# Layer 0 attention: both maxima of a pair of steps ahead of the subtraction, row sums and row of maxima change steps

## The chip, the cores and the metric

The kernel runs on one core of a Trainium2 chip. Its engines work side by side, each through its own queue in order, and meet at semaphores: PE (TensorE) multiplies, VectorE (DVE) and ScalarE (ACT) work on what PE leaves in PSUM, GpSimd (POOL) works in SBUF, SyncE (SP) issues the transfers. The metric is the device time of one execution in microseconds, lower is better.

## The reference

Two layers, each `x = x + attention(layernorm(x)) * silu(ffn(layernorm(x)))`, on x of 2048 tokens by 128. The change touches the attention of layer 0 alone, with 16 heads of 64:

```python
q = jnp.einsum('bsm,hmd->bhsd', x, kernel[0])      # k, v alike
scores = jnp.einsum('bhsd,bhtd->bhst', q, k) * scale
attn = jax.nn.softmax(scores, axis=-1)
out = jnp.einsum('bhst,bhtd->bhsd', attn, v)
out = jnp.transpose(out, (0, 2, 3, 1)).reshape(b, s, d * h)
out = jnp.einsum('bsf,fm->bsm', out, WO[0])
```

The softmax subtracts from each row of 2048 scores its maximum.

## The kernel before, in words

The two layers run one after the other, each as a chain of stages. `attention_stage` (from line 565) is the stage of the attention, for layer 0 with `bias=False` and for layer 1 with `bias=True`. It works in 64 chunks n: 16 heads of 4 chunks, each with 512 query columns. A chunk is 8 steps s; a step takes 256 keys as two blocks of 128, each 128 x 512 scores in one half of a PSUM tile `st` (two such tiles, used in turn).

The exact maximum of each query row has to be known before its scores are made. So the kernel makes the scores twice. Two chunks ahead (`AHEAD = 2`), a cheap product `maxima(n + 2, s)` (PE, lines 652 and 653) fills the one buffer `jb`, and VectorE reduces it to one maximum per row (line 845). PE may not fill `jb` again until the reduction has read it. At the start of chunk n VectorE's `merge(n + 1)` (line 851) joins the partial maxima; ScalarE's `divide_maxima(n + 1)` (line 772), issued after the exponential of step 2, spreads them into `m4w`; PE's `row(n + 1)` (line 663) turns `m4w` into a row of maxima in the PSUM tile `xb`; ScalarE copies that to `rows` (line 777), where the scores of chunk n + 1 find it.

Within a chunk the scores (line 688) of even steps carry the maximum as a fourth pair of products, and ScalarE takes the exponential straight from PSUM (line 795). For odd steps VectorE subtracts the maximum (`subtract_maxima`, line 865) into the ring `prob` (`room`, six tiles), and ScalarE takes the exponential there (line 788). PE's `values` (line 699), two steps behind, multiply the exponentials with v into `ov`. GpSimd adds up the exponentials for the sum of each row (lines 943, 946, 950), which ends in `total`.

The finish of a chunk runs in the next one, all of it through the one tile `xb`: ScalarE copies `ov` out (line 802, after the exponential of step 1); PE's `sums_of` (line 710) sums `total` over the partitions, VectorE inverts (line 884); PE's `project` (line 719) multiplies with the output weights, and VectorE accumulates into `acc` (line 890). In which step these stand is set by `SUM_STEP`, `ROW_STEP` and `OUT_STEP`, whose first number is that of layer 0: sums at step 3, row at step 5, projection at step 7.

PE's queue of layer 0 goes by pairs of steps, and `between` holds the row, the sums or the projection:

```python
elif s % 2 == 0:
    ahead(n, s)
    scores(n, s)
    scores(n, s + 1)
    ahead(n, s + 1)
    between(n, s + 1)
if s % 2 == 0 and step >= LAG:
    values(*divmod(step - LAG, NS))
    values(*divmod(step - LAG + 1, NS))
```

Of the kernel before, what the change touches and what calls it, by code (L numbers as in the profile page):

```python
# [19 lines left out]
NCH = H * NC  # L20
# [14 lines left out]
BW = S - P + S - QC + QC  # L35
AHEAD = 2
NJ = 8
SUM_STEP, ROW_STEP, OUT_STEP = (3, 3), (5, 1), (7, 5)


class Memory:
# [523 lines left out]
def attention_stage(nc, k, layer, bias=False):  # L565

    with ExitStack() as ctx:
# [23 lines left out]
        row_ready, row_done = m.sem(g + "row_ready"), m.sem(g + "row_done")  # L591
# [4 lines left out]
        sum_ready, rs_done = m.sem(g + "sum_ready"), m.sem(g + "rs_done")  # L596
# [10 lines left out]
        def scratch(n, j):  # L607
            i = NJ * n + j
            return jb[:, :] if i >= FIRST or i % 3 == 2 else st[:, i % 3, :]

        def summed_by(step):
            n, s = divmod(step, NS)
            return pool_adds * n + (1, 1, 2, 2, 3, 4, 5, 6)[s]

        def by_row(step):
            return bias or step % 2 == 0

        @block.sync
        def _(sp):
            for h in range(H):  # L620
                if h >= 1:
                    sp.wait_ge(loaded, 16 * loads * h)
                    sp.wait_ge(low_loaded, 16 * 4 * h)
                if h >= 2:
                    sp.wait_ge(st_read, NS * NC * (h - 1))
                at = slice((h % 2) * S, (h % 2 + 1) * S)
                pr, half = h // 2, slice((h % 2) * DH, (h % 2 + 1) * DH)
                for low in (slice(0, DH), slice(DH, P)):
                    sp.dma_start(qh[low, at], k.qk_high[0, pr][half, :]).then_inc(loaded, 16)
                    sp.dma_start(kh[low, at], k.qk_high[1, pr][half, :]).then_inc(loaded, 16)  # L630
                if bias:
                    sp.dma_start(tab[:, h % 2, :], k.bias_rows(h)).then_inc(loaded, 16)
                if h == 0:
                    sp.wait_ge(loaded, 16 * loads)
                for low in (slice(0, DH), slice(DH, P)):
                    sp.dma_start(ql[low, at], k.qk_low[0, pr][half, :]).then_inc(low_loaded, 16)
                    sp.dma_start(kl[low, at], k.qk_low[1, pr][half, :]).then_inc(low_loaded, 16)

        @block.tensor
        def _(pe):  # L640
# [14 lines left out]

            def row(n):
                pe.wait_ge(m4_done, n + 1)
                if bias and n >= 3:
                    pe.wait_ge(proj_done, n - 2)
                if not bias and n >= 2:  # L660
                    pe.wait_ge(rs_done, n - 1)
                for t in range(4):
                    last = nc.tensor.matmul(xb[:, t * P:(t + 1) * P], m4w[:, t, :], k.ident16[:, :],
                                            start=True, stop=True)
                last.then_inc(row_ready, 1)
# [37 lines left out]

            def sums_of(n):
                pe.wait_ge(folded, n + 1)
                pe.wait_ge(row_done, min(n + (3 if bias else 2), NCH))
                if n >= 1:
                    pe.wait_ge(proj_done, n)
                for q in range(4):
                    last = nc.tensor.matmul(xb[:, q:q + 1], total[:, q * P:(q + 1) * P], k.ones[:, 0:1],  # L710
                                            start=(q == 0), stop=True, skip_group_check=True)
                last.then_inc(sum_ready, 1)
# [11 lines left out]
            for j in range(NJ):  # L724
                maxima(0, j)
            row(0)
            for j in range(NJ):
                maxima(1, j)
# [31 lines left out]
            for s in range(NS - LAG, NS):  # L760
                values(NCH - 1, s)
            sums_of(NCH - 1)
            project(NCH - 1)

# [66 lines left out]
        @block.vector  # L831
        def _(ve):
            def maxima(n, j):
                ve.wait_ge(max_ready, NJ * n + j + 1)
                if bias:
                    i = NJ * n + j
                    if i >= 2:
                        ve.wait_ge(max_done, i - 1)
                    c0 = 2 * QC + (n % NC) * QC + (j // 2) * P - (j % 2) * 2 * QC
                    nc.vector.tensor_tensor_reduce(  # L840
                        out=junk[:, i % 2, :], in0=scratch(n, j), in1=tab[:, n // NC % 2, c0:c0 + 2 * QC][:, ::-1], scale=1.0,
                        scalar=-3.0e38, op0=ALU.add, op1=ALU.max, accum_out=mx[:, j // 2, j % 2:j % 2 + 1])\
                      .then_inc(max_done, 1)
                else:
                    nc.vector.reduce_max(mx[:, j // 2, j % 2:j % 2 + 1], scratch(n, j), AX.X).then_inc(max_done, 1)  # L845

            def merge(n):
                ve.wait_ge(max_done, NJ * n + NJ)
                if n >= 1:
                    ve.wait_ge(m4_done, n)  # L850
                nc.vector.tensor_reduce(m4[:, :], mx[:, :, :], AX.X, ALU.max).then_inc(merged, 1)
                ve.wait_ge(merged, n + 1)

            def subtract_maxima(n, s):
                step = NS * n + s
                ve.wait_ge(st_ready, step + 1)
                if s == 1:
                    ve.wait_ge(row_done, n + 1)
                if step >= RING:
                    ve.wait_ge(pv_done, step - RING + 1)  # L860
                    ve.wait_ge(summed, summed_by(step - RING))
                p = prob[:, step % RING, :].rearrange("p (t q) -> p t q", t=2)
                x = st[:, step % 2, :].rearrange("p (t q) -> p t q", t=2)
                high = rows[:, n % 2, :].unsqueeze(1).broadcast_to([P, 2, QC])
                nc.vector.scalar_tensor_tensor(p, high, -float(MAXROW), x, ALU.mult, ALU.add).then_inc(lowered, 1)  # L865

            def add_bias(n, s):
                step = NS * n + s
                ve.wait_ge(st_ready, step + 1)
                if step >= RING:  # L870
                    ve.wait_ge(pv_done, step - RING + 1)
                    ve.wait_ge(summed, summed_by(step - RING))
                c0 = S - QC + 2 * s * P - (n % NC) * QC
                first = tab[:, n // NC % 2, c0:c0 + QC]
                window = bass.AP(first.tensor, first.offset, [first.ap[0], [P, 2], [1, QC]])
                p = prob[:, step % RING, :].rearrange("p (t q) -> p t q", t=2)
                x = st[:, step % 2, :].rearrange("p (t q) -> p t q", t=2)
                nc.vector.tensor_tensor(p[:, :, ::-1], x[:, :, ::-1], window, ALU.add).then_inc(added, 1)  # L878

            def invert(n):  # L880
                ve.wait_ge(sum_ready, n + 1)
                if n >= 1:
                    ve.wait_ge(proj_done, n)
                nc.vector.reciprocal(rs[:, :], xb[:, 0:4]).then_inc(rs_done, 1)

            def accumulate(n):
                ve.wait_ge(proj_ready, n + 1)
                for q in range(4):
                    a = k.acc[:, (n % NC) * 4 + q, :]
                    last = nc.vector.scalar_tensor_tensor(a, xb[:, q * P:(q + 1) * P], rs[:, q:q + 1], a,  # L890
                                                          ALU.mult, ALU.add)
                last.then_inc(proj_done, 1)

            ve.wait_ge(ones_set, 2)
            for j in range(NJ):
                maxima(0, j)
            merge(0)
            for j in range(NJ):
                maxima(1, j)
            for n in range(NCH):  # L900
                if n + 1 < NCH:
                    merge(n + 1)
                for s in range(NS):
                    if bias:
                        add_bias(n, s)
                    if not by_row(NS * n + s):
                        subtract_maxima(n, s)
                    if n + AHEAD < NCH:
                        maxima(n + AHEAD, s)
                    if s == sum_step and n >= 1:  # L910
                        invert(n - 1)
                    if not bias and s == out_step and n >= 1:
                        accumulate(n - 1)
            invert(NCH - 1)
            if not bias:
                accumulate(NCH - 1)
# [462 lines left out]
```

## Time and profile before

| | |
|---|---|
| median of the runs before | 3075.92 us (3074.8 to 3075.96) |
| the profiled execution | 3079.59 us, its span 3077.9 us, mean granted clock of PE 0.964 |
| busy over the span | PE 91%, VectorE 81%, GpSimd 81%, ScalarE 51% |
| attention of layer 0 | about 201 to 1431 us, chunk after chunk 18.6 us |
| busy in 300 to 400 us, of 100 | PE 97.88, VectorE 83.40, GpSimd 94.82, ScalarE 56.68; granted clock 1.00 |

A row of the timeline is: start, duration, engine, line, operation, tiles written and read, count, and in brackets the idle time of the engine before it with what ended it. Instructions of an engine follow one another a little faster than their durations say, since the end of one overlaps the start of the next; so intervals are read from start to start. Several rows of PE overlap because two products on different halves of the array run together and are pipelined.

### The profile page before, as it was taken

What the parts mean: (1) busy time and instruction counts of PE and PEld (TensorE: products, weight loads), DVE (VectorE), ACT (ScalarE), POOL (GpSimd) and SP (SyncE); (2) the same over time, 40 slices, a digit from 0 to 9 for tenths busy, and PEclk for the clock granted to TensorE, in tenths of its full rate; (3) what the DMA queues carried; (4) which work ended last, traced back from release to release, by engine and by line L of the source; (5) the groups of instructions that cost most, each with busy time, mean ns of one, the idle gap of its engine ahead of it and who ended that gap; (6) DMA issues with size and microseconds to landing.
All of it is one profiled execution on the core that took longest, in us unless ns stands there. A gap on an engine that the chain in (4) does not pass through costs nothing. (4 is left out here: it accounts for less than half of the span.)

```text
span 3077.9 us, 46733 instructions
## 1 busy us (share of the span) xinstructions
PE 2807.8 (91%) x17656; PEld 1147.6 (37%) x17656; DVE 2504.0 (81%) x3379; ACT 1557.4 (51%) x1889; POOL 2502.6 (81%) x1205
## 2 busy tenths in 40 slices
PE   5959999999999999996499599999999999999997
PEld 3413333333333333333354133333333333333332
DVE  6568888888888888874339699999999999999995
ACT  4325555555555555552122255555555555555554
POOL 0009999999999999994339389999999999999997
PEclk9979999999999999997699699999999999999998
DMA  4250111111111111101203501111111111111100
GB/s 109 86 191 22 35 29 28 28 28 28 28 28 28 28 29 28 28 1 38 60 27 137 190 4 52 55 55 55 55 55 55 55 55 55 55 55 55 55 1 14
DMA packets 63825, 155.28 MB, mean 50 GB/s; under 512 B 18017, under 2 KB 33770, under 8 KB 61426
## 3 DMA queue, kind: packets, MB, share of 16 engines
q1 hardware_dynamic: 62578, 150.20, 17.4%
q8 instruction: 141, 2.31, 0.3%
q0 software_dynamic: 1024, 2.10, 0.2%
q14 instruction: 82, 0.67, 0.1%
HBM read 113.34 MB, written 38.93 MB: 49 GB/s over the span
## 5 line engine op out<-in xcount | busy, mean ns | idle before, releaser
L943 POOL TENSOR_TENSOR a_sums<-a_sums,room 128x1024 f32<-128x1024 f32 x512 | 1195.4, 2364 | 83.1 <-ACT room L795 42.5
L699 PE MATMUL a_ov<-room,va 128*64 128x512 f32 x4096 | 994.0, 606 | 0.0
L784 ACT ACTIVATE room<-room,sscale 128x1024 f32<-128x1024 f32 x512 | 588.3, 1149 | 539.3 <-DVE room L878 539.2
L845 DVE TENSOR_REDUCE a_mx<-a_jb 128x1 f32<-128x1024 f32 x501 | 611.9, 1221 | 129.6 <-PE a_jb L653 123.4
L943 POOL TENSOR_TENSOR a_sums<-room 128x1024 f32<-128x1024 f32 x256 | 604.3, 2361 | 116.6 <-ACT room L784 66.8
L840 DVE CUSTOM_DVE_ANT_0 a_junk<-a_jb,a_tab 128x1024 bf16<-128x1024 f32 x501 | 610.5, 1219 | 83.2 <-PE a_jb L653 74.8
L878 DVE TENSOR_TENSOR room<-a_st,a_tab 128x1024 f32<-128x1024 f32 x512 | 622.9, 1217 | 12.4 <-PE a_st L688 10.2
L795 ACT ACTIVATE room<-a_st,sscale 128x1024 f32<-128x1024 f32 x256 | 285.3, 1114 | 360.1 <-PE a_st L688 360.1
L652 PE MATMUL a_jb<-a_kh,a_qh 64*128 64x512 f16 x1002 | 384.9, 384 | 66.1 <-DVE a_mx L840 32.1
L699 PEld LDWEIGHTS a_ov<-room,va 128*64 128x64 f32 x4096 | 248.7, 136 | 409.3 <-issue 372.7
L688 PE MATMUL a_st<-a_qh,a_kh 64*128 64x512 f16 x2048 | 395.6, 383 | 3.0 <-DVE a_mx L840 2.9
L688 PE MATMUL a_st<-a_ql,a_kh 64*128 64x512 f16 x2048 | 390.8, 378 | 0.0
L688 PE MATMUL a_st<-a_qh,a_kl 64*128 64x512 f16 x2048 | 390.6, 378 | 0.0
L865 DVE SCALAR_TENSOR_TENSOR room<-a_rows,a_st 128x1024 f32<-128x1024 f16 x256 | 312.7, 1221 | 92.3 <-PE a_st L688 90.9
L653 PE MATMUL a_jb<-a_kh,a_qh 64*128 64x512 f16 x1002 | 385.1, 384 | 0.0
L788 ACT ACTIVATE room<-room,sscale 128x1024 f32<-128x1024 f32 x256 | 294.0, 1148 | 170.8 <-DVE room L865 170.8
L946 POOL TENSOR_TENSOR a_sums<-a_sums 128x1024 f32<-128x1024 f32 x128 | 302.8, 2366 | 10.1
L688 PE MATMUL a_st<-a_rows,a_lower 64*128 64x512 f16 x1536 | 292.9, 378 | 0.0
L652 PEld LDWEIGHTS a_jb<-a_kh,a_qh 64*128 64x128 f16 x1002 | 93.6, 93 | 465.8 <-DVE a_mx L845 306.3
L688 PEld LDWEIGHTS a_st<-a_qh,a_kh 64*128 64x128 f16 x2048 | 99.8, 94 | 274.0 <-issue 164.1
L950 POOL TENSOR_TENSOR a_total<-a_sums 128x512 f32<-128x512 f32 x128 | 162.5, 1270 | 10.0
L710 PE MATMUL a_xb<-ones,a_total 128*128 128x1 f32 x1024 | 136.4, 254 | 17.3 <-POOL a_total L950 17.3
(219 smaller groups left out, 2642.6 us busy)
## 6 DMA issues: line engine op xcount, KB each, us to landing
a_tab<-bias_line SPq DMA_DIRECT2D x16, 1984.0 KB, 11.0
qk_high<-q_oh SPq DMA_DIRECT2D x32, 512.0 KB, 2.6
qk_low<-q_ol SPq DMA_DIRECT2D x32, 512.0 KB, 3.6
a_qh<-qk_high SPq DMA_DIRECT2D x64, 256.0 KB, 4.5
a_kh<-qk_high SPq DMA_DIRECT2D x64, 256.0 KB, 5.1
a_ql<-qk_low SPq DMA_DIRECT2D x64, 256.0 KB, 7.5
a_kl<-qk_low SPq DMA_DIRECT2D x64, 256.0 KB, 7.8
ex_w<-in_L_ffn_W SPq DMA_DIRECT2D x1, 2048.0 KB, 10.5
```

The source lines that it names most:

```text
L652: nc.tensor.matmul(o[:, 0:QC], qh[0:DH, q0:q0 + P], kh[0:DH, k0:k0 + QC], start=True, stop=True)
L653: nc.tensor.matmul(o[:, QC:2 * QC], qh[DH:P, q0:q0 + P], kh[DH:P, k0 + QC:k0 + 2 * QC], start=True, stop=True).then_inc(max_ready, 1)
L688: last = nc.tensor.matmul(st[:, step % 2, t * QC:(t + 1) * QC], w, x, start=(r == 0), stop=(r == len(rounds) - 1))
L699: last = nc.tensor.matmul(ov[t * DH:(t + 1) * DH, :], k.va[:, 2 * s + t, h * DH:(h + 1) * DH], prob[:, step % RING, t * QC:(t + 1) * QC], ...
L784: nc.scalar.activation(prob[:, r, :], prob[:, r, :], ACT.Exp, scale=k.sscale[:, layer:layer + 1])\
L788: nc.scalar.activation(prob[:, r, :], prob[:, r, :], ACT.Exp, scale=k.sscale[:, 0:1])\
L840: nc.vector.tensor_tensor_reduce(out=junk[:, i % 2, :], in0=scratch(n, j), in1=tab[:, n // NC % 2, c0:c0 + 2 * QC][:, ::-1], scale=1.0, sc ...
L845: nc.vector.reduce_max(mx[:, j // 2, j % 2:j % 2 + 1], scratch(n, j), AX.X).then_inc(max_done, 1)
L865: nc.vector.scalar_tensor_tensor(p, high, -float(MAXROW), x, ALU.mult, ALU.add).then_inc(lowered, 1)
L878: nc.vector.tensor_tensor(p[:, :, ::-1], x[:, :, ::-1], window, ALU.add).then_inc(added, 1)
L943: nc.gpsimd.tensor_tensor(a, first, prob[:, step % RING, :], ALU.add).then_inc(summed, 1)
L946: nc.gpsimd.tensor_tensor(a, a, sums[:, (n + 1) % 2, :], ALU.add).then_inc(summed, 1)
```

## The change

Three things in layer 0. The constants swap the steps of the sums and of the row: sums in step 5, row in step 3. On VectorE both reductions of a pair of steps go ahead of the pair's subtraction. And the waits that keep the shared tile `xb` free are adapted to the new order: the row waits for the accumulation three chunks back (as in layer 1), and the sums wait for the copy of one more row. Layer 1 is the same as before, since its order on VectorE has no subtraction.

```diff
-SUM_STEP, ROW_STEP, OUT_STEP = (3, 3), (5, 1), (7, 5)
+SUM_STEP, ROW_STEP, OUT_STEP = (5, 3), (3, 1), (7, 5)
...
             def row(n):
                 pe.wait_ge(m4_done, n + 1)
-                if bias and n >= 3:
+                if n >= 3:
                     pe.wait_ge(proj_done, n - 2)
-                if not bias and n >= 2:
-                    pe.wait_ge(rs_done, n - 1)
...
             def sums_of(n):
                 pe.wait_ge(folded, n + 1)
-                pe.wait_ge(row_done, min(n + (3 if bias else 2), NCH))
+                pe.wait_ge(row_done, min(n + 3, NCH))
...
                 for s in range(NS):
                     if bias:
                         add_bias(n, s)
+                    if n + AHEAD < NCH:
+                        maxima(n + AHEAD, s)
                     if not by_row(NS * n + s):
                         subtract_maxima(n, s)
-                    if n + AHEAD < NCH:
-                        maxima(n + AHEAD, s)
                     if s == sum_step and n >= 1:
                         invert(n - 1)
```

## Rows read from the trace of the kernel before

**Rows 1.** Waits, 252 to 1380 us: engine, line, releaser: total us, times, longest

```profile
PE a_jb L652 <- DVE a_mx L845: 18.9, 60, 0.3
```

**Rows 2.** Timeline of one chunk, its steps 0 to 3 (616.5 to 625.7 us)

```profile
616.50 0.39 PE L652 MATMUL a_jb<-a_kh,a_qh 64*128 64x512 f16 x1
...
618.44 1.22 DVE L865 SCALAR_TENSOR_TENSOR room<-a_rows,a_st 128x1024 f32<-128x1024 f16 x1 [0.22 <-PE a_st L688]
...
619.58 1.22 DVE L845 TENSOR_REDUCE a_mx<-a_jb 128x1 f32<-128x1024 f32 x1
619.70 1.15 ACT L788 ACTIVATE room<-room,sscale 128x1024 f32<-128x1024 f32 x1 [0.79 <-DVE room L865]
620.75 0.58 ACT L802 ACTIVATE a_osb<-a_ov 128x512 f32<-128x512 f32 x1
...
620.85 0.39 PE L652 MATMUL a_jb<-a_kh,a_qh 64*128 64x512 f16 x1 [0.32 <-DVE a_mx L845]
...
622.15 1.12 ACT L795 ACTIVATE room<-a_st,sscale 128x1024 f32<-128x1024 f32 x1 [0.82 <-PE a_st L688]
...
622.59 0.38 PE L652 MATMUL a_jb<-a_kh,a_qh 64*128 64x512 f16 x1
...
622.90 1.05 PE L710 MATMUL a_xb<-ones,a_total 128*128 128x1 f32 x8
623.16 0.62 ACT L772 ACTIVATE a_m4w<-a_m 128x512 f16<-128x512 f32 x1
```

**Rows 3.** Timeline of the same chunk, steps 4 to 7, and the next chunk's start

```profile
625.75 0.39 PE L652 MATMUL a_jb<-a_kh,a_qh 64*128 64x512 f16 x1
...
626.19 1.22 DVE L845 TENSOR_REDUCE a_mx<-a_jb 128x1 f32<-128x1024 f32 x1 [0.94 <-PE a_jb L653]
...
627.80 0.40 PE L663 MATMUL a_xb<-ident,a_m4w 128*128 128x128 f16 x4
628.13 1.94 PE L699 MATMUL a_ov<-room,va 128*64 128x512 f32 x8
...
630.11 0.39 PE L652 MATMUL a_jb<-a_kh,a_qh 64*128 64x512 f16 x1
...
633.24 1.94 PE L699 MATMUL a_ov<-room,va 128*64 128x512 f32 x8
...
634.32 1.12 DVE L890 SCALAR_TENSOR_TENSOR acc<-a_xb,a_rs,acc 128x128 f32<-128x128 f32 x4
635.11 0.39 PE L652 MATMUL a_jb<-a_kh,a_qh 64*128 64x512 f16 x1
...
635.36 0.15 DVE L851 TENSOR_REDUCE a_m<-a_mx 128x4 f32<-128x8 f32 x1
635.61 1.23 DVE L845 TENSOR_REDUCE a_mx<-a_jb 128x1 f32<-128x1024 f32 x1
```

**Rows 4.** Timeline near the stage's end: ScalarE's copy and the exponential behind it

```profile
1383.90 0.58 ACT L802 ACTIVATE a_osb<-a_ov 128x512 f32<-128x512 f32 x1
...
1384.38 1.11 ACT L795 ACTIVATE room<-a_st,sscale 128x1024 f32<-128x1024 f32 x1
```

**Rows 5.** Timeline of the stage's start: the first division and the row behind it

```profile
211.07 0.63 ACT L772 ACTIVATE a_m4w<-a_m 128x512 f16<-128x512 f32 x1 [23.77 <-DVE a_m L851]
...
211.75 0.61 PE L663 MATMUL a_xb<-ident,a_m4w 128*128 128x128 f16 x4 [3.70 <-ACT a_m4w L772]
```

**Rows 6.** Timeline of PE in the last chunk of the stage

```profile
1406.01 1.05 PE L710 MATMUL a_xb<-ones,a_total 128*128 128x1 f32 x8 [1.87 <-POOL a_total L950]
1406.99 2.60 PE L699 MATMUL a_ov<-room,va 128*64 128x512 f32 x8
...
1412.12 1.94 PE L699 MATMUL a_ov<-room,va 128*64 128x512 f32 x8
...
1415.60 1.16 PE L719 MATMUL a_xb<-wo,a_osb 128*128 128x128 f32 x8
```

**Rows 7.** Busy by stretch: PE, PEld, DVE, ACT, POOL, then granted clock, DMA, GB/s

```profile
1409.00:1410.00 1.00, 1.00 (x6) 0.21 (x6) 0.00 (x0) 0.00 (x0) 1.00 (x1) 0.50 0.00 0
```

## The prediction

> **What bounds the kernel now.** I read the views in this order: the busy shares by stretch (table), then who waits for whom, then one chunk of layer 0 in order of time. A chunk n is 8 steps; I call its four pairs of steps A (0, 1), B (2, 3), C (4, 5) and D (6, 7), and M the product for a row of maxima that PE makes two chunks ahead and VectorE reduces. In the stretch from 300 to 400 us PE is busy for 97.9 us, GpSimd for 94.8, VectorE for 83.4, ScalarE for 56.7 (table). So PE is first in line, and the question for any change here is what PE waits for. What it visibly waits for is M's one buffer: 18.9 us in 60 waits, a third of a us each, until the reduction before has read it [rows 1].
>
> The timeline shows where. The pairs of the chunk start at 616.50 (A), 620.85 (B), 625.75 (C), 630.11 (D), and the next A at 635.11 [rows 2, 3]: 4.35, 4.90, 4.36 and 5.00 us, 18.61 in all. D and B are PE from end to end; B carries the row sums, D the projection. A ends by VectorE: its subtraction starts at 618.44, the reduction of M(1) behind it at 619.58, lasts 1.22 and ends at 620.80, and PE starts B at 620.85 [rows 2]. C, with the row of maxima, is about even. What the change can win is therefore the little by which A (and barely C) is longer than PE's own work.
>
> **The order on VectorE.** Nothing is added or removed: per pair the queue goes from reduce(s), subtract(s+1), reduce(s+1) to reduce(s), reduce(s+1), subtract(s+1). Steps take these intervals, all start to start: subtraction to reduction 1.14 (618.44 to 619.58) [rows 2]; I take the same for reduction to reduction and reduction to subtraction, bounded by 1.14 and the reduction's full 1.22. PE's M to its reduction 0.44 (625.75, 626.19) [rows 3]; end of a reduction to the next M 0.05 (620.80, 620.85) [rows 2]; start of the subtraction to the exponential of that step 1.26 (618.44, 619.70) [rows 2].
>
> Pair A after the change, counted from its first M at 0. In D the accumulation now comes after reduce(7) and subtract(7). PE's M(7) starts 1.74 into a pair (620.85, 622.59) [rows 2], so reduce(7) at 2.18, subtract(7) at 3.32, accumulation at 4.46, merge 1.04 later at 5.50 (634.32, 635.36), reduce(0) 0.25 later at 5.75 (635.36, 635.61) [rows 3]. D lasts 5.00, so reduce(0) starts at 0.75 in A, where it starts at 0.50 now. It ends at 1.97, M(1) goes out at 2.02, the values 0.31 later at 2.33, and the next pair 1.87 behind the values (633.24, 635.11) [rows 3]: B starts at 4.20, not 4.35. The gain is 0.15.
>
> The price is on the other output of the queue. Reduce(1) starts at 2.46, subtract(1) at 3.60 (now 1.94), the exponential of step 1 at 4.86 (now 3.20). ScalarE takes its work in order: behind that exponential stand the copy of the output, the exponential of step 2 and the division of the maxima of chunk n+1 by 128, which makes m4w.
>
> **The row of maxima, from step 5 to step 3.** Moved are four products (0.33 us, 627.80 to 628.13) [rows 3] and ScalarE's copy to a_rows (0.58, beside other work). The row reads m4w, and m4w is made at step 2. In the old place it is ready at 623.16 + 0.62 = 623.78 and read at 627.80, four us later [rows 2, 3]. In the new place PE reaches it at the time of the old row sums, 622.90 [rows 2], before m4w is there. With nothing else changed that is a wait of 0.93. With the new VectorE order it is longer, since ScalarE comes late to step 2: exponential(1) at 4.86, copy 1.05 later (619.70, 620.75) [rows 2] at 5.91, exponential(2) 0.48 later (1383.90, 1384.38; upper bound the copy's full 0.58) [rows 4] at 6.39 instead of 4.20 + 1.30 = 5.50, division 1.01 later (622.15, 623.16) [rows 2] at 7.40, done at 8.02, seen by PE 0.05 later (211.07 + 0.63 = 211.70, PE at 211.75) [rows 5] at 8.07.
>
> PE meanwhile: B starts at 4.20; reduce(2) waits for subtract(1) to leave VectorE, 3.60 + 1.14 = 4.74, ends at 5.96, M(3) at 6.01, and 0.31 later (622.59, 622.90) [rows 2], at 6.32, PE stands at the row. It waits from 6.32 to 8.07: 1.75 us. Queued behind the row on PE are the values of pair A, then all of pair C, so nothing of PE's covers this wait, and GpSimd and VectorE only get slack from it. Then the row, 0.33, at 8.40 the values, 1.87: C starts at 10.27. B takes 6.07 instead of 4.90.
>
> **The row sums, from step 3 to step 5.** Eight PE instructions, and VectorE's reciprocal of 0.17, which sits between a subtraction and the next reduction where VectorE now idles. C takes the 4.90 that B took, ending at 15.17. The new wait of the sums for the copy of the row of n+1 costs nothing: that copy comes behind exponential(3). Subtract(3) starts 1.14 behind reduce(3), reduce(3) at 6.01 + 0.44 = 6.45, so subtract at 7.59, exponential at 8.85, copy at 9.90, done 10.48; PE reaches the sums at 10.27 + 2.05 = 12.32. For the projection in D the reciprocal is in time (subtract(5) at 13.59, reciprocal at 14.73, projection at 15.17 + 2.04 = 17.21). GpSimd's last addition of a chunk waits for the sums of the chunk before; it starts near the end of the next chunk's pair A or in B, while those sums have left in C before it. So that wait is idle too, and the move takes the sums a pair's length away from GpSimd's total, which is what would otherwise stall PE here, since the later exponential(3) also makes GpSimd's second addition late. No DMA is issued by any moved step, and SyncE's waits are on exponentials a whole head back.
>
> **The sum.** D stays 5.00. New chunk: 4.20 + 6.07 + 4.90 + 5.00 = 20.17 against 18.61, so 1.56 more. Of the 64 chunks 62 have both maxima ahead and a row to make; the first of them has no output to copy, so 61 count: 61 x 1.56 = 95 us. The tail of the stage (last two chunks, no M) I take as unchanged: its first chunk has a row that waits, as its sums do now, and the end is GpSimd's. The profiled execution took 3079.59 us (span 3077.9 and 1.7 around it); 3079.6 + 95 = 3174.6 and, since the median of the runs is 3.7 below it, 3171. The bounds of the intervals (1.14 or 1.22 three times in ScalarE's chain, 0.48 or 0.58 once) add at most 0.3 a chunk; overlaps that I count too long would take as much: 3155 to 3187 for this case.
>
> **Rivals.**
> (1) The clock. Now PE has no wait over 0.4 us in the loop and is granted 1.00 (table). At the end of layer 0 it waits 1.87 us before the row sums, and then the stretch 1409 to 1410 shows 0.50 [rows 7], that is 1.2 GHz instead of 2.4: values and the next scores take 1406.99 to 1412.12, 5.13 us, against 1412.12 to 1415.60, 3.48, behind it [rows 6]: 1.65 lost. The new wait of 1.75 is as long. It speaks against a drop that the products behind it are the row and the values, whereas behind the 1.87 came the one-column products of the sums. If every chunk loses 1.65: 3171 + 101 = 3272; if one in two, 3221. The Trainium skill, page "TensorE: Matmul & The Clock Gate", section "A second HAM failure mode: psum-queue depth-cycling", tells of a kernel in which short idle times between groups of matmuls, repeated each iteration, made the clock oscillate; by that rule this rival would be the likeliest, at 3221 to 3272. The rows here show such a drop once or twice, not in a loop.
> (2) ScalarE isn't late. If exponential(2) still starts 1.30 into B (the copy slipping elsewhere, or the subtraction running earlier than I think), the division is done at 4.20 + 1.30 + 1.01 + 0.62 = 7.13 and PE waits 0.86, not 1.75: 1.56 - 0.89 = 0.67 a chunk, 41 us, 3117. Against it: each instruction of the chain is on one in-order engine.
> (3) The other side, faster: the wait for m4w vanishes and only the gain in A and C is left. Then B is 2.12 + 0.33 + 1.87 = 4.32 and the chunk 4.20 + 4.32 + 4.90 + 5.00 = 18.42, 0.19 less, 12 us: 3064. It decides where m4w is ready by 6.32, that is, if ScalarE divides 1.7 us earlier than its queue allows by my intervals; for it speaks only that ScalarE is busy little more than half of the time.
> (4) No change to be seen: the wait shrinks to about 0.2.
>
> **How the numbers follow.** The forecast 0.62; the clock 0.20 (half of it at or below 3225, where only some chunks lose it); ScalarE in time 0.10; faster 0.06; no change 0.02. A range from 3110 to 3225 holds the forecast, rival 2 and the lighter half of rival 1, 0.82. The smallest difference that a measurement of this kernel tells from none is about 0.2%, 6 us: faster 0.06, same 0.02, slower 0.92.
>
> **What would show it.** In the waits of PE a new line, row L663 for ScalarE's a_m4w, some 61 times and near 107 us in total; PE's waits for reductions at M gone or under 0.1 each. In a chunk, B near 6.1 us and A near 4.2; the exponential of step 1 at about 4.9 into the chunk and the division at 7.4; ScalarE's wait for the subtraction about 2.5 in pair A instead of 0.8. The granted clock 1.00 throughout; any 0.50 in the loop is rival 1. If the division is in its old place and the wait is near 0.9, it is rival 2. The prediction is wrong altogether if PE's wait at the row is missing, or if PE waits anew at the sums for GpSimd.

## The result, and the profile after

The changed kernel takes 3159.6 us (median of 4 runs, 3157.0 to 3160.9) against 3075.9 us for the kernel before (4 runs): a ratio of 1.027, 95% interval 1.0252 to 1.0288. It is 84 us slower; forecast were 95.

The busy share of each engine in 100 us of layer 0 fell together, which says that the same work is spread over longer chunks. Columns: PE, weight loads, VectorE, ScalarE, GpSimd, then the granted clock, the DMA share and GB/s. For the same stretch of the kernel before see the table above (PE 97.88).

```profile
300.00:400.00 100.00, 91.56 (x622) 36.28 (x618) 76.79 (x90) 51.88 (x56) 88.16 (x40) 1.00 0.19 43
```

The waits of the changed kernel between 252 and 1440 us (engine, line, releaser: total us, times, longest):

```profile
ACT room L786 <- DVE room L863: 440.0, 237, 2.5
...
PE a_xb L661 <- ACT a_m4w L770: 98.1, 59, 1.7
...
PE a_jb L652 <- DVE a_mx L843: 0.2, 1, 0.2
```

Of PE's 60 waits for VectorE of [rows 1] one is left, and 59 waits for `m4w`, 1.66 us each, have come. That line did not exist in the loop before. ScalarE's waits for the subtraction are now 1.86 us in the mean and up to 2.5. The same line of the kernel before, 252 to 1380 us, has 0.66 in the mean and 0.8 at most:

```profile
ACT room L788 <- DVE room L865: 160.2, 243, 0.8
```

For step 1 alone the bracket was 0.79 in [rows 2] and is 2.33 below.

One chunk of the changed kernel in order of time, which answers to [rows 2] and [rows 3]. Its pairs A, B, C, D start at 640.28, 644.39, 650.42, 655.32, the next chunk at 660.33:

```profile
640.28 0.39 PE L652 MATMUL a_jb<-a_kh,a_qh 64*128 64x512 f16 x1
...
640.74 0.15 DVE L849 TENSOR_REDUCE a_m<-a_mx 128x4 f32<-128x8 f32 x1
640.92 1.22 DVE L843 TENSOR_REDUCE a_mx<-a_jb 128x1 f32<-128x1024 f32 x1
...
642.63 1.22 DVE L843 TENSOR_REDUCE a_mx<-a_jb 128x1 f32<-128x1024 f32 x1 [0.49 <-PE a_jb L653]
...
643.77 1.21 DVE L863 SCALAR_TENSOR_TENSOR room<-a_rows,a_st 128x1024 f32<-128x1024 f16 x1
644.39 0.39 PE L652 MATMUL a_jb<-a_kh,a_qh 64*128 64x512 f16 x1
...
645.01 1.15 ACT L786 ACTIVATE room<-room,sscale 128x1024 f32<-128x1024 f32 x1 [2.33 <-DVE room L863]
...
646.07 0.58 ACT L800 ACTIVATE a_osb<-a_ov 128x512 f32<-128x512 f32 x1
646.17 0.39 PE L652 MATMUL a_jb<-a_kh,a_qh 64*128 64x512 f16 x1
...
646.55 1.10 ACT L793 ACTIVATE room<-a_st,sscale 128x1024 f32<-128x1024 f32 x1
...
647.55 0.62 ACT L770 ACTIVATE a_m4w<-a_m 128x512 f16<-128x512 f32 x1
...
648.23 0.40 PE L661 MATMUL a_xb<-ident,a_m4w 128*128 128x128 f16 x4 [1.66 <-ACT a_m4w L770]
648.55 1.94 PE L697 MATMUL a_ov<-room,va 128*64 128x512 f32 x8
...
650.42 0.39 PE L652 MATMUL a_jb<-a_kh,a_qh 64*128 64x512 f16 x1
```

Read it down ScalarE's column: exponential of step 1, copy of the output, exponential of step 2, division, each straight behind the last, without a bracket after the first. The first began when VectorE's subtraction (643.77), now behind the second reduction, was done. PE put out its last M at 646.17 (0.39 us long) and then waited 1.66 us, until 648.23. Of 60 intervals from one division to the next, 59 are 20.05 or 20.06 us and one is 20.26, against 18.61 before.

### The profile page after: what moved, and what is told of

It reads as the page before. It is cut to its first block and busy times, and to the rows that moved or that the text cites. A ratio compares the mean times of both kernels' runs of the same rounds, so it can differ in the third digit from the quotient of the medians.

```text
span 3157.9 us, 46732 instructions
## 1 busy us (share of the span) xinstructions
PE 2807.4 (89%) x17656; PEld 1146.2 (36%) x17656; DVE 2497.0 (79%) x3379; ACT 1550.5 (49%) x1889; POOL 2507.2 (79%) x1205
## 5 line engine op out<-in xcount | busy, mean ns | idle before, releaser
L717 PE MATMUL a_xb<-wo,a_osb 128*128 128x128 f32 x1024 | 150.1, 290 | 0.6 <-issue 0.6
```

## The experiments

All times are medians, with the kernel before timed on the same chip beside them (3074 to 3076 us); gains and losses are counted from that time. The length of a chunk is the distance from one division of the maxima to the next. Three theories were set against each other: (1) the loss is PE's wait for `m4w` at the row, and VectorE's new order makes ScalarE late to it; (2) the new order costs by itself, through late exponentials that hold GpSimd and the ring; (3) the move of the row alone is the loss.

### The steps alone

```diff
 # changed kernel, VectorE's queue
-                    if n + AHEAD < NCH:
-                        maxima(n + AHEAD, s)
                     if not by_row(NS * n + s):
                         subtract_maxima(n, s)
+                    if n + AHEAD < NCH:
+                        maxima(n + AHEAD, s)
```

> The changed kernel with VectorE's order as before: only the row of maxima (to step 3) and the row sums (to step 5) are moved. Theory 1 (PE waits at the row for m4w, and the new VectorE order makes ScalarE late to it): the row's wait is the short one, 0.95 us in a chunk instead of 1.66, the chunk 19.4 us instead of 20.05, so 3160 - 61 x 0.65 = 3120 us. Theory 2 (the later exponentials of the new order are the loss, through GpSimd and the ring of six tiles, whatever PE waits for at the row): with the old order no loss, 18.6 us a chunk, 3076 us. Theory 3 (the move of the row is all of the loss, the order harmless): 20.0 us, 3160 us.

Measured: 3122.9 us (ratio 1.016, 1.0143 to 1.0177), chunks of 19.44 us. The wait at the row is 0.87 us (waits of PE, 300 to 1300 us):

```profile
PE a_xb L661 <- ACT a_m4w L770: 45.0, 52, 0.9
PE a_jb L652 <- DVE a_mx L843: 16.3, 52, 0.3
```

Theory 1 names the time within 3 us. Theory 3 falls: the move is a little over half of the loss.

### The order alone

```diff
 # kernel before, VectorE's queue
+                    if n + AHEAD < NCH:
+                        maxima(n + AHEAD, s)
                     if not by_row(NS * n + s):
                         subtract_maxima(n, s)
-                    if n + AHEAD < NCH:
-                        maxima(n + AHEAD, s)
```

> The kernel before with VectorE's new order alone; sums in step 3, row in step 5 as before. Theory 1: the row finds m4w ready, but the second addition of GpSimd comes later with the later exponential of step 3, so its total is late for the sums in step 3: PE waits 0.9 us a chunk at the sums, the chunk takes 19.25 us, 3115 us. Theory 2: all of the loss, 20.0 us a chunk, 3160 us. Theory 3: no loss, 18.4 us, 3064 us.

Measured: 3191.3 us (1.0381, 1.0363 to 1.0398). This is slower than the whole change, which no theory had said. The expected wait is there at its expected size, 1.05 us 49 times in 300 to 1300 us:

```profile
PE a_xb L710 <- POOL a_total L950: 51.4, 49, 1.1
```

What was not expected stands behind it. Apart from the first three, the intervals come in two lengths: of 60, 23 take 19.2 to 19.5 us and 37 take 21.1 to 21.3. In a long one (timeline of PE, then busy by stretch with the granted clock third from the end):

```profile
618.69 1.05 PE L710 MATMUL a_xb<-ones,a_total 128*128 128x1 f32 x8 [1.04 <-POOL a_total L950]
619.67 3.63 PE L699 MATMUL a_ov<-room,va 128*64 128x512 f32 x8
623.24 0.39 PE L652 MATMUL a_jb<-a_kh,a_qh 64*128 64x512 f16 x1
```

```profile
619.00:620.00 1.00, 1.00 (x9) 0.95 (x10) 1.00 (x2) 0.26 (x1) 1.00 (x1) 0.86 0.00 0
620.00:621.00 1.00, 1.00 (x4) 0.24 (x2) 0.13 (x2) 0.92 (x1) 0.95 (x1) 0.50 0.00 0
```

The clock falls to 1.2 GHz right behind the sums, and the values take 3.57 us from start to start instead of 1.87. That is 1.7 us a time, the price of rival 1, in a place where the prediction had not looked. A long chunk takes 1.65 us more than a short one: 37 x 1.65 = 61 us of the 117 lost. The short chunks are 0.84 us longer than the 18.61 before, which is the wait: 60 x 0.84 = 50 us. So the row sums cannot stay in their old place once VectorE has the new order.

The kernel before shows such a drop behind almost the same wait, in the last chunk but one of the stage. There the sums waited 1.11 us, the next stretches were granted 0.50, and the values behind them took 3.15 us instead of 1.94. The prediction read only the later drop, behind 1.87 us [rows 6]:

```profile
1386.09 1.05 PE L710 MATMUL a_xb<-ones,a_total 128*128 128x1 f32 x8 [1.11 <-POOL a_total L950]
1387.07 3.15 PE L699 MATMUL a_ov<-room,va 128*64 128x512 f32 x8
```

```profile
1388.00:1389.00 1.00, 1.00 (x4) 0.24 (x2) 0.00 (x0) 0.00 (x0) 1.00 (x2) 0.50 0.07 16
```

### The division early

```diff
 # changed kernel, ScalarE's queue
-                    if s == (0 if bias else 2) and n + 1 < NCH:
+                    if s == 0 and n + 1 < NCH:
                         divide_maxima(n + 1)
```

> The changed kernel, with ScalarE's division of the maxima issued behind the exponential of step 0 instead of step 2; nothing else. Theory 1: m4w is ready 3 us before PE reaches the row, the row's wait is gone, the chunk takes PE's own work plus 0.2 us: 18.3 us, 3160 - 61 x 1.75 = 3053 us, faster than the kernel before. Theory 2: the VectorE order still costs, above 3076 us. Theory 3 gives the same as theory 1.

Measured: 3053.6 us (0.9931, 0.9915 to 0.9948), chunks of 18.33 us. One instruction moved by two steps on ScalarE turns the loss of 84 us into a gain of 21. In its timeline `m4w` is made 3.3 us before PE reads it, and PE's row has no bracket:

```profile
607.00 0.62 ACT L770 ACTIVATE a_m4w<-a_m 128x512 f16<-128x512 f32 x1
...
610.59 0.39 PE L652 MATMUL a_jb<-a_kh,a_qh 64*128 64x512 f16 x1
...
610.91 0.40 PE L661 MATMUL a_xb<-ident,a_m4w 128*128 128x128 f16 x4
```

Theory 2 falls: the subtraction of step 1 is as late here as in the changed kernel (3.50 us into the chunk, against 3.49), and the loss is gone. That does not make the new order free everywhere; the last kernel below takes it back in pair D and gains.

### The old order in pair A alone

```diff
 # changed kernel, VectorE's queue
+                    ahead_first = bias or s >= 2
-                    if n + AHEAD < NCH:
+                    if ahead_first and n + AHEAD < NCH:
                         maxima(n + AHEAD, s)
                     if not by_row(NS * n + s):
                         subtract_maxima(n, s)
+                    if not ahead_first and n + AHEAD < NCH:
+                        maxima(n + AHEAD, s)
```

> The changed kernel, but in the pair of steps 0 and 1 VectorE subtracts ahead of the second reduction, as before; the three other pairs keep the new order. Theory 1: it is the exponential of step 1 that makes ScalarE late, so the row's wait shrinks to 0.95 us as with the steps alone, 19.4 us a chunk, 3119 us. Theory 2: the order costs in every pair, so a quarter of its share comes back: near 3150 us. Theory 3: 3160 us.

Measured: 3123.9 us (1.0161, 1.0144 to 1.0178), chunks of 19.44 us, PE's wait 0.86 us (44.1 us in 51). It equals the steps alone. Of the four places where the order changed, only the one ahead of step 1's exponential feeds the wait.

### The division at steps 1 and 3

```diff
 # changed kernel, ScalarE's queue; 1 in one kernel, 3 in the other
-                    if s == (0 if bias else 2) and n + 1 < NCH:
+                    if s == (0 if bias else 1) and n + 1 < NCH:
                         divide_maxima(n + 1)
```

> The changed kernel with the division behind the copy of the output in step 1, between the two places already measured (step 0: 3054 us, step 2: 3160 us). The wait at the row is set by ScalarE's place for the division alone: 0.7 us a chunk, the chunk 19.05 us, 3099 us.

Measured: 3095.3 us (1.0066, 1.0046 to 1.0086), chunks of 19.05 us, PE's wait 0.66 us (34.9 us in 53).

> The changed kernel with ScalarE's division behind the exponential of step 3 instead of step 2, which makes the wait at the row much longer. PE waits 4.25 us a chunk instead of 1.66; the chunk 22.55 us, 3312 us, if the granted clock stays at 1.00 in the loop. If a wait by itself brings the clock down once it is long enough, the stretch behind the row shows 0.50 and up to 1.7 us a chunk come on top: up to 3415 us.

Measured: 3406.0 us (1.1076, 1.1054 to 1.1098). Chunks of 23.9 to 24.2 us, but for two of 25.4. PE waits 4.15 us, and the clock is down behind the wait (timeline of PE, then the stretch):

```profile
615.46 0.61 PE L661 MATMUL a_xb<-ident,a_m4w 128*128 128x128 f16 x4 [4.15 <-ACT a_m4w L770]
616.00 3.08 PE L697 MATMUL a_ov<-room,va 128*64 128x512 f32 x8
```

```profile
615.00:616.00 1.00, 0.54 (x5) 0.35 (x5) 0.00 (x0) 0.40 (x1) 1.00 (x1) 0.50 0.98 201
```

Set side by side, the same kernel with ScalarE's division in four places:

| division behind | PE's wait at the row | chunk | time | clock in the loop |
|---|---|---|---|---|
| step 0 | none | 18.33 us | 3053.6 us | 1.00 |
| step 1 | 0.66 us | 19.05 us | 3095.3 us | 1.00 |
| step 2 (the change) | 1.66 us | 20.05 us | 3159.6 us | 1.00 |
| step 3 | 4.15 us | 23.9 us | 3406.0 us | 0.50 behind each wait |

From row to row the chunk grows by the wait, 0.72 for 0.66 and 1.00 for 1.00, until the clock joins in: the last step adds 2.49 us of wait and 3.85 us of chunk.

### The row behind the values

```diff
 # changed kernel, PE's queue
                         ahead(n, s + 1)
-                        between(n, s + 1)
+                        if s != 2:
+                            between(n, s + 1)
                     if s % 2 == 0 and step >= LAG:
                         values(*divmod(step - LAG, NS))
                         values(*divmod(step - LAG + 1, NS))
+                        if not bias and s == 2:
+                            between(n, s + 1)
```

> The changed kernel with PE's row put behind the two values of its pair instead of ahead of them; ScalarE and VectorE as in the changed kernel. Theory 1: the values (1.87 us) go into the wait of 1.66 us, m4w is there when PE reaches the row, and the chunk falls to 18.5 us (the values themselves may wait 0.2 us for ScalarE's late copy of the output): 3066 us. If the loss were in the order of VectorE rather than in what PE waits for, the chunk would stay near 20 us, 3160 us.

Measured: 3071.1 us (0.9986, 0.9976 to 0.9995), chunks of 18.62 us, 0.1 more than expected. ScalarE is as late as in the changed kernel (it waits 2.33 or 2.34 us for the subtraction of step 1); only what PE does meanwhile differs. The wait at the row is gone, and the 0.2 us of waiting for ScalarE's copy is there:

```profile
PE a_ov L697 <- ACT a_osb L803: 12.4, 54, 0.2
```

### The sums behind the values, and wide sums

The first kernel makes the same edit of PE's queue as above on the kernel with the order alone. The second leaves that queue and widens the products of the sums:

```diff
 # order alone, sums_of, layer 0
-                    last = nc.tensor.matmul(xb[:, q:q + 1], total[:, q * P:(q + 1) * P], k.ones[:, 0:1],
+                    last = nc.tensor.matmul(xb[:, q * P:(q + 1) * P], total[:, q * P:(q + 1) * P], k.ones[:, :],
...
-                nc.vector.reciprocal(rs[:, :], xb[:, 0:4]).then_inc(rs_done, 1)
+                nc.vector.reciprocal(rs[:, :], xb[:, 0:QC:P]).then_inc(rs_done, 1)
```

> VectorE's new order alone, with PE's row sums put behind the two values of their pair instead of ahead of them. The values (1.87 us) cover the wait of 1.04 us for GpSimd's total; no wait, so no drop of the clock: the chunk near 18.5 us, 3069 us. That would show that the loss of the order alone (117 us) is the wait at the sums and what the clock adds to it. If the later exponentials cost by themselves, the time stays above 3090 us.

Measured: 3072.1 us (0.9992, 0.9982 to 1.0001), chunks of 18.62 us, no wait at the sums in the loop. All 117 us of the order alone are gone, with VectorE's order untouched.

> VectorE's new order alone, as in the run that took 3191 us, but each product of the row sums is made 128 columns wide instead of one (all columns hold the same sum, the reciprocal reads every 128th). There the granted clock fell behind the wait of 1.04 us at the sums in about two of three chunks (21.09 us against 19.45). If it takes the one-column products behind the wait, the clock stays at 1.00 and every chunk takes 19.55 us: 3191 - 39 x 1.65 + 61 x 0.1 = 3133 us. If the wait alone does it, the drops stay: 3195 us.

Measured: 3137.2 us (1.020, 1.0183 to 1.0217). Of the same 60 intervals 57 take 19.5 to 19.6 us and none is longer than 19.8. (The 39 long chunks of the expectation are 37 when counted over the whole stage, which makes its sum 3136.) The wait is the same 1.05 us as with narrow sums, and the granted clock stays:

```profile
PE a_xb L714 <- POOL a_total L954: 53.8, 51, 1.1
```

```profile
300.00:400.00 100.00, 94.59 (x638) 37.12 (x636) 79.23 (x97) 52.75 (x56) 90.46 (x42) 1.00 0.20 43
```

More work on PE, 54 us less. A wait of 1.05 us alone does not bring the clock down here; the same wait together with one-column products behind it does.

That holds for this wait only. At the end of the stage the same kernel waits longer at its wide sums, and there the clock falls (timeline of PE, then the stretch):

```profile
1462.57 1.16 PE L714 MATMUL a_xb<-ones,a_total 128*128 128x128 f32 x8 [1.87 <-POOL a_total L954]
1463.66 3.48 PE L699 MATMUL a_ov<-room,va 128*64 128x512 f32 x8
```

```profile
1464.00:1465.00 1.00, 1.00 (x4) 0.24 (x2) 0.00 (x0) 0.00 (x0) 1.00 (x2) 0.50 0.00 0
```

It falls in the same way behind waits of 2.18 us (at 1442.55) and 2.75 us (at 248.01). So wide products did not keep the clock up behind waits of 1.87 us and more.

### A faster version

```diff
 # division behind step 0, and VectorE's old order in pair D
+                    ahead_first = bias or s < 6
```

> The kernel with the division behind step 0, and VectorE's old order in the last pair (steps 6 and 7) alone. There the projection makes PE the slower one, so the new order wins nothing, and it delays the accumulation and with it the first reduction of the next chunk. Expected: the first pair falls from 4.11 to 4.0 us, the chunk from 18.33 to 18.1, 3040 us. If the new order were of use in the last pair too, the time would rise above 3054 us.

Measured: 3044.9 us (0.9899, 0.9883 to 0.9916), chunks of 18.18 us, 30 us faster than the kernel before. The expectation was 18.1 and 3040; the first pair takes 3.98 us as expected. PE's waits for VectorE and ScalarE are gone from the loop and it is busy throughout:

```profile
600.00:700.00 100.00, 100.00 (x686) 39.95 (x682) 85.24 (x102) 55.95 (x60) 96.81 (x45) 1.00 0.10 22
```

## Why the prediction was right

The sign, the mechanism and the place were as forecast; the size was 95 us for a measured 84. By its own steps:

- **The gain at M.** Forecast 0.15 us for pair A. Measured 4.35 to 4.11, 0.24. The step that was mis-sized is the start of reduce(0) in A, forecast 0.75 into the pair and found at 0.64 (640.28, 640.92): the merge comes 1.04 behind the accumulation as before, but the reduction only 0.18 behind the merge, not 0.25. The rest is that the accumulation comes 4.43 into D, not 4.46. The 0.1 us runs through subtract(1), 3.49 for 3.60, down to the division.
- **ScalarE's chain.** Forecast for the exponential of step 1, the copy, the exponential of step 2, the division and the row: 4.86, 5.91, 6.39, 7.40, 8.07. Measured from 640.28: 4.73, 5.79, 6.27, 7.27, 7.95. The distances agree within 0.02 us; the whole is 0.12 earlier, from the point above. So the interval of 0.48 behind the copy, taken from one row at the end of the stage, holds, and the upper ends of the bounds were not needed.
- **The wait at the row.** Forecast 1.75, measured 1.66. B took 6.03 for a forecast 6.07. The split into 0.93 of the move and the rest of the order is shown by the steps alone (0.87) and by the old order in pair A (0.86).
- **The row sums in step 5.** Forecast at no cost: C takes 4.90, and PE has no wait for GpSimd in the loop. The prediction's reason, that the later exponential would otherwise make the sums late for PE, is shown by the order alone, where that wait is 1.05 us. What it did not see is that this wait also brings the clock down in two chunks of three.
- **The sum.** 20.05 - 18.61 = 1.44 a chunk for a forecast 1.56. The two profiled executions are 80 us apart (spans 3157.9 and 3077.9), and by GpSimd's totals this is 60 longer chunks, 86 us; 4.3 less in the tail; 2.7 less ahead of the first total, of which 1.9 lie ahead of the first division, where the kernels do the same; and 1 us more behind the stage. The medians differ by 84 because the profiled execution of the kernel before lies 3.7 above its median. The tail was taken as unchanged and is not. GpSimd's last two totals come 17.7 us apart, where they were 19.9 and 19.8: the waits of PE at the sums in the last chunks, such as the 1.87 in [rows 6], and the drop of the clock behind them, went with the move to step 5.
- **Rival 1, the clock,** did not happen: 1.00 throughout the loop, behind waits of 1.66. What the prediction held against it is that the one-column products of the sums followed the wait in [rows 6] and not here. The wide sums bear that out at 1.05 us and contradict it at 1.87: behind the very wait of [rows 6] the clock fell with 128-column products too. So this argument was not enough to rule the rival out for a forecast wait of 1.75. That the measured 1.66, only 0.2 below 1.87, kept the clock was in part luck, and no run varies the wait between the two. The rival was real, but for the neighbouring kernel. The Trainium skill, page "TensorE: Matmul & The Clock Gate", section "A second HAM failure mode: psum-queue depth-cycling", tells of a kernel in which frequent short idle times between groups of matmuls made the clock oscillate; the order alone shows that here (1.04 us, 37 of 60 chunks), the changed kernel and the wide sums show as frequent idle times that do not.
- **Rival 2, ScalarE in time,** fell; its wait of 0.86 is what the kernel with the old order in pair A has, and it takes 3124 us there against the 3117 given. **Rival 3, faster,** needed `m4w` by 6.32 into the chunk; the division early provides it, and 18.33 us and 3054 us came out where 18.42 and 3064 were written.

## What to carry to other kernels

When a step is moved earlier in one engine's queue, find the instruction that produces what it reads and walk that engine's queue back from it: here PE's row met a division that stood behind three ScalarE instructions, the first of which the same change had made late. An engine that is busy half of the time is no cover if its few instructions are queued in the wrong order; moving the producer with the consumer turned 84 us of loss into 21 of gain. And when a reordering delays one output and advances another, look for the reader of each: only one of four swaps fed the wait, and the swap in the last pair was worth undoing (18.33 to 18.18 us a chunk).

## What the runs showed of the hardware

In this stage the granted clock did not go by the length of PE's wait alone. Behind a wait of 1.04 us followed by the eight one-column products of the sums it fell to 0.50 in 37 of 60 chunks. Behind the same wait followed by products of 128 columns it stayed at 1.00, and so it did behind 59 waits of 1.66 us followed by the row's products and the values. Longer waits brought it down behind wide products as well: 1.87, 2.18 and 2.75 us once each in the kernel with wide sums, and 4.15 us in every chunk of the loop with the division at step 3, where none is shorter than 23.9 us and 22.5 were due without a drop. A drop made the chunk 1.65 us longer in the order alone, and mostly 1.35 to 1.65 us with the division at step 3. Why the clock held behind 1.66 us in the loop and fell behind 1.87 us at the stage's end is left open: the two places differ in more than the length of the wait. So is why a drop came in some chunks and not in others with the same wait; no run here tells what decides it.
